# Entry to the scans of a state-space layer: sequences per statistics round, place of a table load, order of the silus

## Chip, cores and metric

The kernel runs on one core of a Trainium2 chip. The metric is the device time of one execution in microseconds, taken as the median of several runs. Engines are named as in the profile: PE (TensorE), DVE (VectorE), ACT (ScalarE), POOL (GpSimd) and SP (the queue that issues most DMAs).

## The reference, cut

16 sequences of 36 image tokens and 77 text tokens, 256 wide. Two layers: attention and a mixture of experts, then a state-space (scan) layer and a quantised feed-forward layer. The change lies where the scan layer begins:

```python
h = h + moe(_layernorm(h))            # L0_ffn: the expert answers are added here
x = _layernorm(h)
xr = x @ in_proj_w.T + in_proj_b
x_in, res = split(xr, 2)
xc = silu(causal_depthwise_conv(x_in, conv_w) + conv_b)      # 4 taps
delta, Bp, Cp = split(xc @ x_proj_w.T + x_proj_b, [64, 80])
delta = softplus(delta @ dt_proj_w.T + dt_proj_b)
dA, dBu = exp(delta * -exp(A_log)), delta * Bp * xc
ys = scan(dA * previous + dBu)                                # along time, 16 states
y = ((ys * Cp).sum(-1) + xc * D_param) * silu(res)
h = h + y @ out_proj_w.T + out_proj_b + x @ skip_proj_w.T + skip_proj_b
h = h + quantised_ffn(_layernorm(h))
```

## The kernel before, in words

Every engine has its own instruction stream, written out by hand, and the streams meet on semaphores; an engine runs its stream strictly in the order of the code. Whatever stands behind a waiting instruction on the same engine waits too.

The scan layer works in 8 groups of GB = 2 sequences (N = 226 columns), each group in 8 chunks of two states. After the experts, eight DMAs on SP bring the expert answers back into `xn2`, four sequences to a pair of DMAs and to a semaphore `gathered`. Then the entry begins:

- DVE (`dve_ssm`, from line 1199) quantises the last weights, then `add_answers` adds the answers of some sequences to `resid` and takes their statistics (lines 1203 and 1205, one pair per sequence); `dve_layernorm` (lines 837 to 852) makes mean and rstd out of them. It needs ACT in the middle: after seven operations ACT does Ln and Exp (`act_rstd`, lines 541 and 543), and then come four more on DVE. The first call covers FIRST_SEQS, four sequences. `normalise(0)` (line 1219) writes the two sequences of group 0 to `xn3`. Then the other twelve (OTHER_SEQS) are added, group 1 is normalised once PE has read group 0, and the second layernorm runs. `shift` (line 1285) is for ACT, which normalises the later groups itself.
- PE (`pe_ssm`) turns the group (L1644), projects it into x and then res (L1654, two halves), convolves x with diagonal matrices (L1664), projects xc to rank, B and C (L1673), and rank to dt (L1680). `spread` (L1691) copies B over the partitions, and `reduce` (L1704, L1709) adds what POOL multiplied.
- ACT (`act_ssm`) copies the turned group (L713), adds the bias into `xpad` (`pad`, L724), makes the silus of res (L733) and xc (L736) in `silus`, copies rank, B and C out (`projections`, L745 and L747), and makes softplus (L754 to L759) and the decays (L768). Silu and Exp/Ln lie in different tables. `silus` asks for the Exp/Ln table at its end (L739); the silu table is loaded in front of the first silu, where the profile shows it as line 733, behind the waits of `silus`.
- SP sends C to DRAM and back, spread over all partitions (`c_rows`, lines 414 and 418), once the second copy of `projections` is there; POOL splits B and C into three bfloat16 parts (L461 to L465) after the fourth, and multiplies states by C (L480, L484) in every chunk.
- DVE makes delta and delta * xc (`steps`, L1225, L1227), the drives (L1234) and the scans (L1244).

In each of the other groups this front work is woven into the chunks of the group before. Only for group 0 it stands alone, and for group 1 its convolution stands in chunk 1 of group 0 (OPENING). The streams of `act_ssm` and `dve_ssm` begin, before the change, like this:

```python
act: turn(0, 0); pad(0); silus(0, 0, first=True); projections(0, 0, first=True)
     act_rstd(act, 4, OTHER_SEQS, load=False); softplus(0); turn(1, 1)
dve: normalise(0); add_answers(OTHER_SEQS); wait_ge(x3T_ps, 1); normalise(1)
     dve_layernorm(dve, 4, OTHER_SEQS); shift; memset of the decays' first column; steps(0, 0)
```

After the scans the feed-forward layer follows: scale of x, rounding and turning, gate and up projections (L1620), scale of the hidden layer, down projections (L1634).

Of the kernel before, what the change touches and what calls it, by code (L numbers as in the profile page):

```python
# [18 lines left out]
B, IMG, TXT, D = 16, 36, 77, 256  # L19
# [19 lines left out]
GB = 2  # L39
# [12 lines left out]
AT_NORMALISE, AT_TURN, AT_IN, AT_PAD = 4, 5, 6, 7  # L52
OPENING = 1
AT_SKIP = (3, 4)
FIRST_SEQS, OTHER_SEQS = slice(0, 2 * GB), slice(2 * GB, B)
BUT_ONE_SEQS, ONE_SEQ = slice(0, B - 1), slice(B - 1, B)
ROUTER_BANKS = (0, 1, 3, 4)
TAIL_SEQS = 4
# [38 lines left out]
def build(nc, a, out):  # L97
    ctx = ExitStack()
    with ctx:
# [3 lines left out]
        def sem(name):  # L103
            return ctx.enter_context(nc.semaphore(name))
# [223 lines left out]
        xpad_ready, res_ready, conv_ps, xc_ready = sem("xpad_ready"), sem("res_ready"), sem("conv_ps"), sem("xc_ready")  # L328
# [207 lines left out]
        def act_rstd(act, turn, seqs=slice(0, B), load=True):  # L536

            if load:
                act.preload_act_table_set("natural_log_exp_and_others")
            act.wait_ge(dve_ln, LN_OPS * turn + LN_VAR)  # L540
            act.activation(lnt[:, 3, seqs], lnt[:, 2, seqs], ACT.Ln).then_inc(act_ln, 1)
            act.wait_ge(act_ln, 2 * turn + 1)
            act.activation(lnt[:, 3, seqs], lnt[:, 3, seqs], ACT.Exp, scale=-0.5).then_inc(act_ln, 1)
# [166 lines left out]
        def act_ssm(act):  # L710
# [10 lines left out]
            def pad(g):  # L721
                act.wait_ge(xin_ps, g + 1)
                for m in range(KT):
                    act.activation(xpad[:, m, :, TAPS - 1:], ps[:, 1, m * N:(m + 1) * N].rearrange("p (b s) -> p b s", b=GB),  # L724
                                   ACT.Identity, bias=in_b[:, m:m + 1]).then_inc(xpad_ready, 1)

            def silus(g, par, first=False):
                act.wait_ge(res_ps, g + 1)
                act.wait_ge(conv_ps, g + 1)
                if not first:  # L730
                    act.wait_ge(yT_ready, g)
                for m in range(KT):
                    act.activation(silu_res[par][:, m, :], ps[:, 0, m * N:(m + 1) * N], ACT.Silu, bias=in_b[:, KT + m:KT + m + 1])\  # L733
                        .then_inc(res_ready, 1)
                for m in range(KT):
                    act.activation(xc[par][:, m, :], ps[:, 1, m * N:(m + 1) * N], ACT.Silu, bias=conv_b[:, m:m + 1])\  # L736
                        .then_inc(xc_ready, 1)

                act.preload_act_table_set("natural_log_exp_and_others")  # L739

            def projections(g, par, first=False):
                act.wait_ge(proj_ps, g + 1)
                if not first:
                    act.wait_ge(c_out, 16 * g)
                act.activation(rankT, ps[0:RANK, 0, 0:N], ACT.Identity, bias=rank_b).then_inc(proj_ready, 1)  # L745
                for dst, rows in ((bc, 96), (bc_hi, 96), (bc3[par], 32)):
                    act.activation(dst[0:rows, :], ps[0:rows, 0, N:2 * N], ACT.Identity, bias=bc_b[0:rows, :]).then_inc(proj_ready, 1)  # L747

            def softplus(g):

                q = Seq(act, sp_step, 5 * g)
                act.wait_ge(dt_ps, g + 1)
                for m in range(KT):
                    q.done(act.activation(sp_abs[:, m, :], ps[:, 1, m * N:(m + 1) * N], ACT.Abs, bias=dt_b[:, m:m + 1]))  # L754
                for m in range(KT):
                    q.done(act.activation(sp_relu[:, m, :], ps[:, 1, m * N:(m + 1) * N], ACT.Relu, bias=dt_b[:, m:m + 1]))
                q.wait()
                q.step(act.activation(sp_abs, sp_abs, ACT.Exp, scale=-1.0))
                act.activation(sp_abs, sp_abs, ACT.Ln, bias=1.0).then_inc(softplus_ready, 1)  # L759
# [37 lines left out]
            turn(0, 0)  # L797
            pad(0)
            silus(0, 0, first=True)
            projections(0, 0, first=True)  # L800
            act_rstd(act, 4, OTHER_SEQS, load=False)
            softplus(0)
            turn(1, 1)
            act.wait_ge(aneg_done, 2)
# [10 lines left out]
        @block.scalar  # L815
        def _(act):
            act_tokens(act)
            act_rstd(act, 0)
            act.wait_ge(clip_in, 2 * 16)
            act.activation(clip_sig[:, :], clips[:, :], ACT.Exp, scale=-1.0).then_inc(clip_exp, 1)  # L820
            act_attention(act)
            act_router(act)
            act_shared(act)
            act_experts(act)
            act_weights_down(act)
            act_rstd(act, 3, FIRST_SEQS)
            act_ssm(act)
            act_rstd(act, 6, LAST_SEQS, load=False)
            act_ffn(act)
# [3 lines left out]
        def dve_layernorm(dve, turn, seqs=slice(0, B)):  # L833

            q = Seq(dve, dve_ln, LN_OPS * turn)
            me, qe, mo, qo = (stats[:, seqs, k] for k in (1, 2, 4, 5))
            q.done(dve.tensor_tensor(lnt[:, 0, seqs], me, mo, ALU.add))
            q.done(dve.tensor_tensor(lnt[:, 1, seqs], me, mo, ALU.subtract))
            q.done(dve.tensor_tensor(lnt[:, 2, seqs], qe, qo, ALU.add))
            q.wait()  # L840
            q.done(dve.tensor_scalar(mean[:, seqs], lnt[:, 0, seqs], 0.5, None, ALU.mult))
            q.done(dve.tensor_scalar(lnt[:, 2, seqs], lnt[:, 2, seqs], 1.0 / D, EPS, ALU.mult, ALU.add))
            q.step(dve.tensor_tensor(lnt[:, 1, seqs], lnt[:, 1, seqs], lnt[:, 1, seqs], ALU.mult))
            q.step(dve.scalar_tensor_tensor(out=lnt[:, 2, seqs], in0=lnt[:, 1, seqs], scalar=0.25, in1=lnt[:, 2, seqs], op0=ALU.mult, op1=ALU.add))
            assert q.n == LN_VAR

            dve.wait_ge(act_ln, 2 * turn + 2)
            y, v, t = lnt[:, 3, seqs], lnt[:, 2, seqs], lnt[:, 4, seqs]
            q.step(dve.tensor_tensor(t, y, y, ALU.mult))
            q.step(dve.tensor_tensor(t, t, v, ALU.mult))  # L850
            q.step(dve.tensor_scalar(t, t, -0.5, 1.5, ALU.mult, ALU.add))
            q.step(dve.tensor_tensor(rstd[:, seqs], y, t, ALU.mult))
            assert q.n == LN_OPS
# [345 lines left out]
        def dve_ssm(dve):  # L1199
            def add_answers(seqs):  # L1200
                for b in range(seqs.start, seqs.stop):
                    dve.wait_ge(gathered[b // 4], 32)
                    dve.tensor_tensor(resid[:, b, :], resid[:, b, :], xn2[:, b, :], ALU.add).then_inc(resid2_ready, 1)
                    dve.wait_ge(resid2_ready, b + 1)
                    dve.bn_stats(stats[:, b, :], resid[:, b, :]).then_inc(stats_done, 1)
                dve.wait_ge(stats_done, 2 * B + seqs.stop)
# [9 lines left out]
            def normalise(g):  # L1216
                for r in range(GB):
                    b = GB * g + r
                    dve.tensor_scalar(xn3[r], resid[:, b, :], mean[:, bass.ds(b, 1)], rstd[:, bass.ds(b, 1)],
                                      ALU.subtract, ALU.mult).then_inc(xn3_ready, 1)  # L1220
# [58 lines left out]
            dve.wait_ge(ey_ps, ETILES)  # L1279
            normalise(0)  # L1280
            add_answers(OTHER_SEQS)
            dve.wait_ge(x3T_ps, 1)
            normalise(1)
            dve_layernorm(dve, 4, OTHER_SEQS)
            dve.scalar_tensor_tensor(out=shift[:, :], in0=mean[:, :], scalar=-1.0, in1=rstd[:, :], op0=ALU.mult, op1=ALU.mult).then_inc(shift_ready, 1)
            dve.wait_ge(wqT_ready, 2 + 2 * FT + 4)
            for n in range(2):
# [13 lines left out]
        @block.vector  # L1301
        def _(dve):
            dve_tokens(dve)
            dve_layernorm(dve, 0)
            dve_attention(dve)
            dve_clips(dve)
            dve_router(dve)
            dve_shared(dve)
            dve_experts(dve)
            dve_ssm(dve)  # L1310
            dve_ffn(dve)
# [559 lines left out]
```

## Time and profile before

| | |
|---|---|
| median of 3 runs | 865.48 us (865.08 to 865.71) |
| the profiled execution | 865.44 us, span 863.5 us |
| mean granted TensorE clock | 0.89 of full speed |
| busy: PE, DVE, ACT, POOL | 699.7, 520.7, 392.2, 351.2 us |

The profile is one execution. Times in it are microseconds from the start of its span; the span is 1.9 us shorter than the execution's own time.
### The profile page before, as it was taken

What the parts mean: (1) busy time and instruction counts of PE and PEld (TensorE: products, weight loads), DVE (VectorE), ACT (ScalarE), POOL (GpSimd) and SP (SyncE); (2) the same over time, 40 slices, a digit from 0 to 9 for tenths busy, and PEclk for the clock granted to TensorE, in tenths of its full rate; (3) what the DMA queues carried; (4) which work ended last, traced back from release to release, by engine and by line L of the source; (5) the groups of instructions that cost most, each with busy time, mean ns of one, the idle gap of its engine ahead of it and who ended that gap; (6) DMA issues with size and microseconds to landing.
All of it is one profiled execution on the core that took longest, in us unless ns stands there. A gap on an engine that the chain in (4) does not pass through costs nothing. (4 is left out here: it accounts for less than half of the span.)

```text
span 863.5 us, 12104 instructions
## 1 busy us (share of the span) xinstructions
PE 699.7 (81%) x3696; PEld 474.2 (55%) x3697; DVE 520.7 (60%) x931; ACT 392.2 (45%) x858; POOL 351.2 (41%) x332
## 2 busy tenths in 40 slices
PE   7699999997999957999994788897788785535958
PEld 5577777775655524665663555455456452213557
DVE  1555555555231102544436568988988988974974
ACT  0465555554422103233222456665665662106973
POOL 0021111110035802323221158878878888420625
PEclk9899999997999968999997789999999997566955
DMA  9990000000002153111114202201210220000002
GB/s 274 335 416 20 0 0 0 0 2 0 1 7 39 31 104 114 44 49 43 43 36 98 88 1 87 87 29 59 86 54 34 87 87 0 0 0 1 0 11 76
DMA packets 28696, 52.73 MB, mean 61 GB/s; under 512 B 10965, under 2 KB 23545, under 8 KB 26489
## 3 DMA queue, kind: packets, MB, share of 16 engines
q1 hardware_dynamic: 19929, 47.49, 16.6%
q0 software_dynamic: 8736, 4.85, 2.2%
q8 instruction: 16, 0.26, 0.1%
q14 instruction: 15, 0.12, 0.0%
HBM read 42.62 MB, written 9.60 MB: 60 GB/s over the span
## 5 line engine op out<-in xcount | busy, mean ns | idle before, releaser
L480 POOL TENSOR_TENSOR arena<-arena 128x904 f32<-128x904 f32 x64 | 124.8, 1953 | 59.3 <-DVE arena L1244 53.0
L1244 DVE TENSOR_TENSOR_SCAN arena<-ps,arena 128x452 f32<-128x452 f32 x128 | 133.5, 1085 | 6.7 <-ACT ps L768 2.1
L768 ACT ACTIVATE ps<-arena,sh_w 128x448 f32<-128x448 f32 x128 | 80.3, 635 | 107.7 <-DVE arena L1244 106.9
L1704 PE MATMUL ps<-arena,const 128*128 128x452 f32 x112 | 63.2, 650 | 41.3 <-POOL arena L484 41.3
L554 ACT ACTIVATE work<-ps,work 113x113 f32<-113x113 f32 x256 | 67.1, 420 | 56.3 <-DVE work L899 56.3
L1528 PE MATMUL ps<-arena,work 128*128 x176 | 86.5, 618 | 0.3 <-issue 0.3
L428 POOL TENSOR_TENSOR xT<-work 128x452 f32<-128x452 f32 x16 | 15.1, 943 | 157.7 <-DVE work L888 157.7
L1234 DVE TENSOR_TENSOR arena<-arena,ps 128x904 f32<-128x904 f32 x64 | 69.2, 1082 | 11.1 <-PE ps L1691 10.7
L511 POOL DMA_INDIRECT slots_in<-xn,slot x16 | 37.9, 2366 | 74.1 <-issue 74.1
L484 POOL TENSOR_TENSOR arena<-arena 128x452 f32<-128x452 f32 x56 | 64.1, 1144 | 4.4
L527 POOL DMA_INDIRECT answers_e<-work,slot_token x22 | 23.7, 1076 | 101.5 <-DVE work L1033 101.5
L1496 PE MATMUL ps<-xT,sh_w 128*128 (+1 forms) x128 | 50.9, 556 | 0.0
L1029 DVE TENSOR_TENSOR work<-ps,work 128x512 f32<-128x512 f32 x22 | 15.2, 691 | 58.5 <-PE ps L1528 58.5
L1704 PEld LDWEIGHTS ps<-arena,const 128*128 128x128 f32 x112 | 19.2, 207 | 53.3 <-POOL arena L484 53.2
L1528 PEld LDWEIGHTS ps<-arena,work 128*128 128x128 f32 x176 | 31.5, 197 | 24.6 <-issue 24.4
L1540 PE MATMUL ps<-arena,work 128*128 x176 | 43.1, 389 | 0.8 <-ACT work L624 0.8
L1377 PE MATMUL ps<-const,work 113*113 113x113 f32 x256 | 37.4, 269 | 5.0 <-ACT work L554 4.7
L1654 PE MATMUL ps<-arena,sh_w 128*128 128x226 f32 x128 | 38.4, 462 | 0.7 <-ACT arena L713 0.7
L1496 PEld LDWEIGHTS ps<-xT,sh_w 128*128 128x128 f32 x128 | 24.9, 196 | 23.7 <-issue 23.2
L899 DVE TENSOR_REDUCE work<-ps 113x4 f32<-113x452 f32 x64 | 35.7, 620 | 2.8 <-PE ps L1371 2.8
L1377 PEld LDWEIGHTS ps<-const,work 113*113 113x113 f32 x256 | 31.6, 178 | 10.1 <-ACT work L554 8.8
L1540 PEld LDWEIGHTS ps<-arena,work 128*128 128x128 f32 x176 | 32.9, 197 | 5.3 <-issue 1.5
(239 smaller groups left out, 1428.5 us busy)
## 6 DMA issues: line engine op xcount, KB each, us to landing
arena<-c_rows SPq DMA_DIRECT2D x8, 1808.0 KB, 6.5
arena<-in_ex_w SPq DMA_DIRECT2D x8, 1536.0 KB, 23.6
slots_in<-work SPq DMA_DIRECT2D x1, 2827.0 KB, 22.3
work<-slots_in SPq DMA_DIRECT2D x22, 128.5 KB, 2.1
xn<-answers_e SPq DMA_DIRECT2D x4, 448.0 KB
out<-resid SPq DMA_DIRECT2D x8, 224.0 KB
arena<-in_patches SPq DMA_DIRECT2D x3, 576.0 KB, 6.0
sh_w<-in_sh_w SPq DMA_DIRECT2D x1, 1536.0 KB, 11.4
```

The lines of the kernel that those rows point to most:

```text
L480: pool.tensor_tensor(read[kp], state[kp], c_all[par][:, 2 * c:2 * c + 2, :].unsqueeze(2).broadcast_to([P, 2, KT, N]), ALU.mult)\
L484: pool.tensor_tensor(read[kp][:, 0], read[kp][:, 0], read[kp][:, 1], ALU.add).then_inc(pair_ready, 1)
L554: last = act.activation(probs[:, r, j], ps[0:S, 3 + r, j * S:(j + 1) * S], ACT.Exp, bias=negmax[:, h:h + 1])
L768: act.activation(decay_ps(n)[:, :, 1:], delta[par].rearrange("p k (b s) -> p (k b) s", b=GB)[:, :, 1:], ACT.Exp, scale=a_neg[:, 2 * c + n: ...
L1234: dve.tensor_tensor(drive[kp], dx[par].unsqueeze(1).broadcast_to([P, 2, KT, N]), ps[:, 2 + kp, 0:2 * N].rearrange("p (n s) -> p n s", n=2) ...
L1244: dve.tensor_tensor_scan(state[kp][:, n].rearrange("p k s -> p (k s)"), decay_ps(n).rearrange("p q s -> p (q s)"), drive[kp][:, n].rearran ...
L1377: last = pe.transpose(ps[0:S, 3 + r, j * S:(j + 1) * S], probs[:, r, j, :], ident[0:S, 0:S])
L1496: last = pe.matmul(ps[:, bank, 0:4 * S], sh_w[:, at + k * HID + m * P:at + k * HID + (m + 1) * P], xT2[:, k, bass.ds(g * 4 * S, 4 * S)], s ...
L1528: last = pe.matmul(ps[:, bank, :], xgT[par][:, k, :], arena[:, bass.ds(e * EW + at + k * HID, HID)], start=k == 0, stop=k == KT - 1)
L1540: last = pe.matmul(ps[:, 6, 0:D], e_hT[:, m, :], arena[:, bass.ds(e * EW + DOWN + m * D, D)], start=m == 0, stop=m == HT - 1)
L1654: last = pe.matmul(ps[:, 1 - m // KT, m % KT * N:(m % KT + 1) * N], in_w[:, k, m * P:(m + 1) * P], x3T[par][:, k, :], start=k == 0, stop=k ...
L1704: pe.matmul(ps[:, 6, 0:KT * N], ident, read[kp][:, 0].rearrange("p k s -> p (k s)"), start=False, stop=False, skip_group_check=True).then_ ...
```

## The change

FIRST_SEQS shrinks from four sequences to the two of group 0, and OTHER_SEQS grows to fourteen. In `silus` of group 0 alone, the silu table is asked for by an instruction of its own ahead of the waits, the silus of res wait for the res projection alone, and the wait for the convolution stands between them and the silus of xc. On ACT, Ln and Exp of the second layernorm move ahead of `projections(0)`. On DVE, the second layernorm moves ahead of `normalise(1)` and its wait.

```diff
-FIRST_SEQS, OTHER_SEQS = slice(0, 2 * GB), slice(2 * GB, B)
+FIRST_SEQS, OTHER_SEQS = slice(0, GB), slice(GB, B)
...
             def silus(g, par, first=False):
+                if first:
+                    act.preload_act_table_set("silu_and_others")
                 act.wait_ge(res_ps, g + 1)
-                act.wait_ge(conv_ps, g + 1)
                 if not first:
+                    act.wait_ge(conv_ps, g + 1)
                     act.wait_ge(yT_ready, g)
                 for m in range(KT):
                     act.activation(silu_res[par][:, m, :], ps[:, 0, m * N:(m + 1) * N], ACT.Silu, bias=in_b[:, KT + m:KT + m + 1])\
                         .then_inc(res_ready, 1)
+                if first:
+                    act.wait_ge(conv_ps, g + 1)
                 for m in range(KT):
                     act.activation(xc[par][:, m, :], ps[:, 1, m * N:(m + 1) * N], ACT.Silu, bias=conv_b[:, m:m + 1])\
                         .then_inc(xc_ready, 1)
...
             silus(0, 0, first=True)
+            act_rstd(act, 4, OTHER_SEQS, load=False)
             projections(0, 0, first=True)
-            act_rstd(act, 4, OTHER_SEQS, load=False)
             softplus(0)
...
             add_answers(OTHER_SEQS)
+            dve_layernorm(dve, 4, OTHER_SEQS)
             dve.wait_ge(x3T_ps, 1)
             normalise(1)
-            dve_layernorm(dve, 4, OTHER_SEQS)
```

## Rows read from the trace of the kernel before

**Rows 1.** The chain of waits around the stall; start us, us, what.

```profile
502.39 5.12 issue
...
512.36 2.10 DVE arena L1244 x2
...
514.52 1.95 POOL arena L480
```

**Rows 2.** The timeline, DVE, 462 to 516 us; start, us, engine, line, operation.

```profile
465.04 0.43 DVE L1203 TENSOR_TENSOR resid<-resid,xn 113x256 f32<-113x256 f32 x1 [2.95 <-DMA xn<-answers_e]
...
468.32 0.17 DVE L837 TENSOR_TENSOR lnt<-stats 113x4 f32<-113x4 f32 x1
...
469.75 0.16 DVE L849 TENSOR_TENSOR lnt<-lnt 113x4 f32<-113x4 f32 x1 [0.58 <-ACT lnt L543]
...
471.05 0.74 DVE L1219 TENSOR_SCALAR arena<-resid,mean,rstd 113x256 f32<-113x256 f32 x2 [0.54 <-DVE rstd L852]
...
480.80 0.43 DVE L1205 BATCH_NORM_STATS2 stats<-resid 113x6 f32<-113x256 f32 x1
...
482.66 0.17 DVE L844 SCALAR_TENSOR_TENSOR lnt<-lnt 113x12 f32<-113x12 f32 x1
...
495.81 2.09 DVE L1244 TENSOR_TENSOR_SCAN arena<-ps,arena 128x452 f32<-128x452 f32 x2
```

**Rows 3.** The timeline, PE, same stretch.

```profile
471.93 0.98 PE L1644 MATMUL ps<-const,arena 113*128 113x113 f32 x4 [6.51 <-DVE arena L1219]
...
479.20 3.22 PE L1664 MATMUL ps<-arena,xT 128*128 128x226 f32 x16
485.31 3.47 PE L1673 MATMUL ps<-arena,sh_w 128*64 128x226 f32 x8 [2.90 <-ACT arena L736]
489.32 1.03 PE L1680 MATMUL ps<-arena,sh_w 64*128 64x226 f32 x4 [0.54 <-ACT arena L745]
...
502.44 5.00 PE L1664 MATMUL ps<-arena,xT 128*128 128x226 f32 x16 [2.61 <-ACT arena L724]
...
510.33 1.92 PE L1673 MATMUL ps<-arena,sh_w 128*64 128x226 f32 x8 [0.40 <-ACT arena L736]
```

**Rows 4.** The timeline, ACT, same stretch.

```profile
477.03 0.79 ACT L724 ACTIVATE arena<-ps,sh_w 128x226 f32<-128x226 f32 x2 [3.47 <-PE ps L1654]
482.50 1.28 ACT L733 ACT_TABLE_LOAD   x1 [4.67 <-PE ps L1664]
...
484.47 0.79 ACT L736 ACTIVATE arena<-ps,sh_w 128x226 f32<-128x226 f32 x2
...
488.82 0.45 ACT L745 ACTIVATE arena<-ps,sh_w 64x226 f32<-64x226 f32 x1 [2.26 <-PE ps L1673]
...
490.17 0.19 ACT L541 ACTIVATE lnt<-lnt 113x12 f32<-113x12 f32 x1
...
490.51 0.77 ACT L754 ACTIVATE arena<-ps,sh_w 128x226 f32<-128x226 f32 x2
```

**Rows 5.** Busy time and granted clock by stretch (PEclk after the POOL column).

```profile
475.20:478.60 3.40, 3.40 (x10) 3.05 (x10) 3.23 (x10) 0.79 (x2) 0.00 (x0) 0.50 0.00 0
478.60:482.00 3.40, 3.40 (x19) 3.35 (x19) 3.26 (x10) 0.00 (x0) 0.00 (x0) 1.00 0.00 0
...
485.40:488.80 3.40, 3.39 (x8) 1.57 (x8) 0.00 (x0) 1.16 (x1) 0.00 (x0) 0.50 0.02 5
```

**Rows 6.** The transfers of C on SP's queue, all groups.

```profile
L418 SPq DMA_DIRECT2D arena<-c_rows x8: 338/338/348, 491.0 to 706.2; - x8
...
DMA to landing us min/median/max: 6.2/6.5/6.8
```

**Rows 7.** Busy time and clock by stretch, hidden layer and end.

```profile
791.70:796.00 4.30, 4.25 (x12) 2.33 (x13) 0.68 (x1) 3.12 (x5) 0.00 (x0) 0.50 0.02 4
796.00:809.70 13.70, 13.36 (x70) 7.96 (x68) 10.96 (x20) 13.42 (x24) 9.13 (x8) 1.00 0.00 1
...
823.40:858.00 34.60, 28.13 (x129) 27.52 (x130) 23.38 (x39) 21.50 (x12) 13.26 (x14) 0.50 0.14 41
```
## The prediction

> **What bounds the kernel now.** I read the chain of waits first. From 514.52 us on, the chain that ends last runs through POOL's products (L480) group after group, and ahead of that there are a few microseconds in which nothing else works: ACT idles 5.12 us until the convolution of group 1 is there, then loads tables and makes silus, and the scans go on at 512.36 [rows 1]. What this chain says for the change: from there on each step is released by the one before it, so whatever brings the first scan forward brings the end forward by as much, if the stall at 502 to 512 moves along. The view does not reach ahead of 502 in detail, so I read the entry (465 to 496 us) engine by engine in the order of time.
>
> DVE [rows 2]: answers of sequences 0 to 3 are added from 465.04; the layernorm over four begins at 468.32, group 0 is normalised at 471.05, twelve more sequences are added until 481.23, and the first seven operations of their layernorm end at 482.83. The first scan starts at 495.81. PE [rows 3]: turns group 0 from 471.93, after 6.51 idle, projects, convolves from 479.20, and waits 2.90 for ACT ahead of the x projection at 485.31. ACT [rows 4]: bias into xpad at 477.03, then 4.67 of idleness until the convolution, then table, four silus, table, and the four bc and rank copies from 488.82. So the entry is one serial path DVE, PE, ACT, PE, ACT, DVE, beside which DVE adds the other sequences. In such a stretch a removed link counts whole, as long as the work beside it is not late.
>
> **The change, part by part.** The entry's path before: 465.04 (add) to 468.32, layernorm, 471.93 (PE), 482.42 (convolution ends), 482.50 table, 483.78 silus of res, 484.47 silus of xc, 485.31 x projection, 488.82 copies, 490.51 softplus, 495.81 first scan.
>
> (a) *Two sequences instead of four.* Four cost 468.32 - 465.04 = 3.28, two leave 1.64 [rows 2]. The layernorm's operations are so small (0.17 for 4 columns, 0.17 for 12) that their width is worth nothing. Gain on the path 1.64. The two moved sequences join the others: 14 x 0.79 = 11.1 us from about 470.1, ending at 481.2, as before, because the normalising of group 0 comes earlier by just what the two cost. The answers wanted first (sequences 0 to 3) came at 465.0, when DVE first stopped waiting, and sequence 4 is wanted at 471.7, as before, so no load comes under pressure.
>
> (b) *The silu table while ACT waits.* The load of 1.28 at 482.50 [rows 4] goes behind the bias copies, which end at 475.4 + 0.8 = 476.2 (1.64 ahead of 477.03 + 0.79). The second half of the projection ends only at about 477.6, so the load is covered by PE. Gain 1.28. If the cover were gone it would cost at most these 1.28. The Trainium skill (ScalarE: Activation LUTs, What ACT_TABLE_LOAD costs) says a switch of set costs about 2.66 us, a drain of 1.38 beside the load of 1.28. The row shows 1.28 from the load's start to the first silu's, since ACT had long been empty; by the page the sum would be 1.38 larger, and the row decides.
>
> (c) *Silus of res during the convolution.* They run from 482.50 + 1.28 = 483.78 to 484.47: 0.69 off the path. They now need the second half of the projection alone and fit beside the 3.2 us of the convolution. They write nothing that it reads. Gain 0.69.
>
> (d) *Ln and Exp ahead of the copies instead of behind.* Before, they stood at 490.17 between the copies and softplus, while PE computed dt until 490.35; softplus began at 490.51. Freed, it can begin at about 490.40: gain 0.1. In the new place ACT waits for DVE's seventh layernorm operation, and behind that wait stand the copies, the SP queue's c_rows transfers, POOL's split of B and C, and softplus. DVE now skips the normalising of group 1 (0.65) before it: seventh operation at about 482.1. ACT gets there after xc (485.26 - 3.61 = 481.65) and the table back (1.28): 482.93. So ACT does not wait; Ln and Exp end at about 483.4, before the x projection (below, 483.6). Cost nothing, while DVE is not later than that.
>
> (e) *Group 1 normalised after the layernorm.* Four operations after Exp take 0.76 (469.75 to 470.51), normalising 0.74 and the 0.54 ahead of it: xn3 is ready near 485.5. PE wants it after dt, near 485.2. A delay of 0.3 there, covered: PE's next work for the scans (B spread over the partitions) waits for POOL's split anyway, 2.5 us more. Cost nothing.
>
> (f) *PE's clock.* Not in the diff, but the gaps between PE's bursts shrink. The granted clock was 1.00 (2.4 GHz) during the convolution, and 0.50 (1.2 GHz) in 485.40 to 488.80, after an idle time of 2.90 [rows 3, 5]. The same x projection shape takes 3.51 until its copy begins at half clock (485.31 to 488.82) and 1.92 later (510.33), which is the pace of the convolution at full clock, 3.22 for 16. With (b) and (c) the idle time ahead of it is 0.06 + 0.79 + 0.04 = 0.9 in place of 2.90; idle times as short as 0.54 ahead of dt left the clock full. Bounds: 0 (it falls all the same) and 1.92 against 3.47 = 1.55. I take 1.55, because 0.9 is much nearer to 0.54 than to 2.90. The projection into x and res ran at half clock from 473.6 to 478.6 [rows 5]; starting 1.64 sooner after the work that ended at 465.42 it may meet the rise at another place. Bounds by what was paid at half clock: 5.0 us at 0.50 cost 2.5, the convolution fully at half would cost 3.0 more. I take 0 and keep some of each.
>
> (g) *The transfer of C* is issued at 491.0 first and lands 6.5 us later [rows 6], 8.7 after the copies start at 488.82; the first scans end 495.81 + 2.09 - 488.82 = 9.1 after. It stays covered by a few tenths.
>
> (h) *The stall at 502 to 512.* Only the first group's order is changed, so it keeps its shape. Its convolution took 5.00 for 16 matmuls against 3.22 for the same 16 at full clock [rows 3]; at half throughout it would be about 6.2. So it can move by -1.8 to +1.2. I take 0.
>
> Sum: 1.64 + 1.28 + 0.69 + 0.10 + 1.55 = 5.26. The profiled execution took 865.44 us (span 863.5), 0.04 under the median of 865.48: **860.2 us**. What a measurement can tell from no change is about 0.2%, 1.7 us.
>
> **The rivals.**
> *Rigid shift.* The clock still falls ahead of the x projection, and (f) gives nothing: 3.7, 861.7 us. For it: what the clock had before is what one execution shows. Against: the short gap. The Trainium skill (TensorE: Matmul & The Clock Gate, Part 1) says that the instants at which activity is judged run free of the program, so other executions can meet them elsewhere; one trace cannot show that. Chance 0.22.
>
> *More clock, until DVE's statistics bind.* If the projection also gets its full clock sooner, the path reaches ACT's Ln before DVE does. Then the copies start at 482.1 + 0.45 = 482.6 at the earliest, 6.2 before 488.82: this is the cap, 6.3 with (d), 859.1 us; with a group 1 convolution at full clock too, up to 1.8 less, 857.3. Chance 0.25.
>
> *Given back.* The clock pattern shifts against the later work: the convolution of group 1 at half throughout (+1.2), or the hidden layer's first stretch, which ran 4.3 us at 0.50 and then at 1.00 [rows 7], rising one or two us later (+0.9). 3.7 - 2.1 = 1.6 gained: 863.8, no measurable change. Chance 0.08.
>
> *Slower.* The hidden layer's stretch from 796.0 to 809.7 ran at 1.00 with PE busy 13.36 of 13.70; the last stretch ran at 0.50 though PE was busy 28.13 of 34.60 [rows 7]. If the shift makes the first one stay at half as well, its 13.4 us of matmuls become 26.8: 865.4 - 5.3 + 13.4 = 873.5. It decides from 5.3 us of full-clock work done at half. For it: the last stretch shows that being busy is not enough. Against: the work itself, which set the rise, is the same. Chance 0.03.
>
> *It does not do what it says.* If a second silu load still stood before the silus, it would fall on those of res and be covered by the convolution (476.2 + 2.56 = 478.8, silus until 479.6, convolution until 480.8): nothing lost; this is inside the first cases.
>
> **How the numbers follow.** The sum as taken 0.42, rigid 0.22, cap 0.25, given back 0.08, slower 0.03. The likeliest gives the time, 860.2. Range 858.0 to 863.0: it takes in most of the cap's case and the rigid one with the conv at half, and leaves out the last two and the far end of the cap's. Faster by over 0.2% (below 863.7): 0.91; within: 0.06; slower: 0.03.
>
> **What would show it.** ACT: a table load right behind the bias copies, silus of res inside the convolution, no load between the convolution and xc. PE: idle under 1 us ahead of the x projection, and 1.7 to 2.0 us for its 8 matmuls. DVE: seventh layernorm operation at 482.0 to 482.3, and ACT's Ln not waiting for it. First scan near 490.6, the resumed scans near 507.1, and all of 514 to 863 shifted by the same. The prediction is wrong if Ln waits over 1 us for DVE, if the clock in the x projection is 0.50, or if the gain at the first scan differs from that at the end by over 1.5 us.

## The result, and the profile after

The change makes the kernel faster by half a per cent. Over 18 runs of each, 863.07 us median (858.09 to 865.01) against 866.75 (865.08 to 869.55), ratio 0.9949 with a 95% interval of 0.9936 to 0.9962, that is 4.4 us (3.3 to 5.5). The two medians are 3.7 apart, which lies in that interval too. The forecast was 5.26 us. Its 860.2 stood on the first three runs of the kernel before (865.48); carried over with the ratio, that is 865.48 x 0.9949 = 861.1. The median of the 18 runs itself lies 0.07 above the upper end of the forecast's range. Both kernels spread more than those three runs showed.

The profiled execution of the changed kernel took 860.82 us, span 859.0 (before: 865.44, span 863.5). ACT in the order of time at the entry, columns as in [rows 4]; lines behind 725 have moved by up to 4:

```profile
468.02 1.28 ACT L539 ACT_TABLE_LOAD   x1
469.32 0.20 ACT L541 ACTIVATE lnt<-lnt 113x2 f32<-113x2 f32 x1
...
477.53 0.79 ACT L724 ACTIVATE arena<-ps,sh_w 128x226 f32<-128x226 f32 x2 [3.47 <-PE ps L1658]
478.33 1.28 ACT L729 ACT_TABLE_LOAD   x1
479.63 0.79 ACT L735 ACTIVATE arena<-ps,sh_w 128x226 f32<-128x226 f32 x2
482.14 0.79 ACT L740 ACTIVATE arena<-ps,sh_w 128x226 f32<-128x226 f32 x2 [1.72 <-PE ps L1668]
482.94 1.28 ACT L743 ACT_TABLE_LOAD   x1
484.31 0.21 ACT L541 ACTIVATE lnt<-lnt 113x14 f32<-113x14 f32 x1
484.56 0.21 ACT L543 ACTIVATE lnt<-lnt 113x14 f32<-113x14 f32 x1
484.93 0.44 ACT L749 ACTIVATE arena<-ps,sh_w 64x226 f32<-64x226 f32 x1 [0.16 <-PE ps L1677]
...
486.49 0.79 ACT L758 ACTIVATE arena<-ps,sh_w 128x226 f32<-128x226 f32 x2
```

The table of silu is loaded right behind the bias copies, the silus of res (479.63) lie inside the convolution, and the silus of xc start 0.04 after it ends, with no load between. The rows below are PE of the same kernel, against [rows 3]:

```profile
472.42 0.99 PE L1648 MATMUL ps<-const,arena 113*128 113x113 f32 x4 [5.05 <-DVE arena L1223]
474.11 4.94 PE L1658 MATMUL ps<-arena,sh_w 128*128 128x226 f32 x16 [0.70 <-ACT arena L713]
478.88 3.22 PE L1668 MATMUL ps<-arena,xT 128*128 128x226 f32 x16
482.98 1.92 PE L1677 MATMUL ps<-arena,sh_w 128*64 128x226 f32 x8 [0.88 <-ACT arena L740]
485.43 1.03 PE L1684 MATMUL ps<-arena,sh_w 64*128 64x226 f32 x4 [0.53 <-ACT arena L749]
486.51 0.61 PE L1648 MATMUL ps<-const,arena 113*128 113x113 f32 x4
...
498.43 4.72 PE L1668 MATMUL ps<-arena,xT 128*128 128x226 f32 x16 [2.88 <-ACT arena L724]
```

The idle time ahead of the x projection is 0.88 instead of 2.90, and its 8 matmuls take 1.92 instead of 3.47. DVE, against [rows 2]:

```profile
466.54 0.43 DVE L1207 TENSOR_TENSOR resid<-resid,xn 113x256 f32<-113x256 f32 x1 [2.79 <-DMA xn<-answers_e]
...
468.92 0.16 DVE L848 SCALAR_TENSOR_TENSOR lnt<-lnt 113x2 f32<-113x2 f32 x1
...
471.54 0.74 DVE L1223 TENSOR_SCALAR arena<-resid,mean,rstd 113x256 f32<-113x256 f32 x2 [0.93 <-DVE rstd L856]
...
484.10 0.17 DVE L848 SCALAR_TENSOR_TENSOR lnt<-lnt 113x14 f32<-113x14 f32 x1
...
485.50 0.17 DVE L856 TENSOR_TENSOR rstd<-lnt 113x14 f32<-113x14 f32 x1
485.71 0.74 DVE L1223 TENSOR_SCALAR arena<-resid,mean,rstd 113x256 f32<-113x256 f32 x2
...
491.80 2.09 DVE L1248 TENSOR_TENSOR_SCAN arena<-ps,arena 128x452 f32<-128x452 f32 x2
```

Three things are new. Between the last operation of group 0's layernorm and its normalising DVE is idle for 0.93, not 0.54. Between the same two operations for group 1 (485.50, 485.71) there is only 0.04. And the seventh operation of the second layernorm ends at 484.27, 0.05 after ACT's table load (482.94 + 1.28 = 484.22) and 0.04 before ACT's Ln: ACT was already there, and DVE released it. The clock by stretch, against [rows 5] (granted clock after the POOL column): the projection's first 3.3 us at half, then full through the convolution and the x projection.

```profile
474.10:477.40 3.30, 3.29 (x9) 2.97 (x10) 3.13 (x10) 0.00 (x0) 0.00 (x0) 0.50 0.00 0
477.40:478.80 1.40, 1.40 (x9) 1.39 (x8) 1.36 (x4) 1.26 (x3) 0.00 (x0) 0.99 0.00 0
478.80:484.90 6.10, 5.22 (x26) 3.94 (x24) 5.19 (x20) 4.11 (x8) 0.00 (x0) 1.00 0.02 3
```

The differences of starts in the two profiles, step by step, are the whole balance:

| from, to | before | after | gained | forecast |
|---|---|---|---|---|
| first add, normalising of group 0 | 6.01 | 5.00 | 1.01 | 1.64 |
| normalising, projection | 2.56 | 2.57 | 0 | 0 |
| projection, convolution | 5.59 | 4.77 | 0.82 | 0 (bounds -3.0, +2.5) |
| convolution, x projection | 6.11 | 4.10 | 2.01 | 1.97 |
| x projection, copies | 3.51 | 1.95 | 1.56 | 1.55 |
| copies, softplus | 1.69 | 1.56 | 0.13 | 0.10 |
| softplus, first scan | 5.30 | 5.31 | 0 | 0 |
| **entry: first add, first scan** | **30.77** | **25.26** | **5.51** | **5.26** |
| first scan, resumed scans | 16.55 | 16.27 | 0.28 | 0 |
| resumed scans, end | 351.14 | 350.93 | 0.21 | 0 |

One more term lies ahead of the entry, where the code is the same: the first add came at 466.54 instead of 465.04, 1.50 later. 5.51 + 0.28 + 0.21 - 1.50 = 4.50, the difference of the spans.

The chain of waits after looks as in [rows 1], 4.3 us earlier (start us, us, what). So the gain of the entry passed through the stall into the scans:

```profile
498.38 4.84 issue
503.23 1.28 ACT L735
...
508.07 2.10 DVE arena L1248 x2
...
510.24 1.95 POOL arena L480
```

### The profile page after: what moved, and what is told of

It reads as the page before. It is cut to its first block and busy times, and to the rows that moved or that the text cites. A ratio compares the mean times of both kernels' runs of the same rounds, so it can differ in the third digit from the quotient of the medians.

```text
span 859.0 us, 12103 instructions
## 1 busy us (share of the span) xinstructions
PE 699.3 (81%) x3696; PEld 474.8 (55%) x3697; DVE 519.9 (61%) x931; ACT 393.1 (46%) x858; POOL 350.6 (41%) x332
## 5 line engine op out<-in xcount | busy, mean ns | idle before, releaser
L1658 PE MATMUL ps<-arena,sh_w 128*128 128x226 f32 x128 | 36.2, 440 | 0.7 <-ACT arena L713 0.7
```

## The experiments

The questions were: what each part is worth by itself, whether it is the idle time that takes PE's clock, why the first step fell short, and whether DVE's statistics are the next bound. The entry's length comes from one profile per run, with no noise from the code ahead of it. It is the sharper measure beside the times. "Filler" below means matmuls added on PE whose result is not used.

**e1_two_seqs.** The kernel before, with only the number of first sequences changed.

```diff
-FIRST_SEQS, OTHER_SEQS = slice(0, 2 * GB), slice(2 * GB, B)
+FIRST_SEQS, OTHER_SEQS = slice(0, GB), slice(GB, B)
```

> The kernel before with FIRST_SEQS = 2 sequences alone. The measure is the entry: from DVE's first add of answers to the first scan, 30.77 us before and 25.26 after the whole change. Theory (two sequences are 1.64 on the path): entry 29.1, time 1.6 below the kernel before. Rival (ACT's weight copies and its table load stand behind the same arrival and cap the gain, since the changed kernel went from the first add to group 0's normalising in 5.00 us against 6.01): entry 29.8, 1.0 below. The clock ahead of the x projection should be 0.50 again, 3.5 us for it.

Ratio 0.9991 (0.9974 to 1.0007), no measurable change. From the first add (464.93) to the normalising it took 4.80, and the entry took 30.30. DVE and PE:

```profile
469.73 0.73 DVE L1219 TENSOR_SCALAR arena<-resid,mean,rstd 113x256 f32<-113x256 f32 x2 [0.93 <-DVE rstd L852]
```

```profile
472.29 6.15 PE L1654 MATMUL ps<-arena,sh_w 128*128 128x226 f32 x16 [0.70 <-ACT arena L713]
...
484.39 3.08 PE L1673 MATMUL ps<-arena,sh_w 128*64 128x226 f32 x8 [2.90 <-ACT arena L736]
488.01 1.87 PE L1680 MATMUL ps<-arena,sh_w 64*128 64x226 f32 x4 [0.54 <-ACT arena L745]
```

The step paid 1.21, not 1.64, and of that PE's clock took most back. The whole projection ran at half (6.15 for 16 against 5.75 before) and so did dt (1.87 against 1.03), while the x projection came out 0.39 shorter; the entry kept 0.47. The rival blamed ACT's load. That load ended at 467.40, before DVE's seventh operation (467.47), and Ln started 0.03 after the latter, so the load was in time here and is not the cause. The missing 0.43 is, but for 0.04, the growth of the idle time from 0.54 to 0.93. The time alone can't tell the theory (1.6) from the rival (1.0).

**e2_silus.** The kernel before, with only the new `silus`: early table, silus of res ahead of the wait for the convolution.

```diff
+                if first:
+                    act.preload_act_table_set("silu_and_others")
                 act.wait_ge(res_ps, g + 1)
-                act.wait_ge(conv_ps, g + 1)
                 if not first:
+                    act.wait_ge(conv_ps, g + 1)
                     act.wait_ge(yT_ready, g)
...
+                if first:
+                    act.wait_ge(conv_ps, g + 1)
```

> The kernel before with the table asked for early and the silus of res during the convolution, four first sequences kept, and Ln/Exp and layernorm in their old places. Theory (removed 1.28 + 0.69 on ACT, and PE's clock stays full in the x projection, 1.55 more): entry 27.2 us, idle time ahead of the x projection 0.9 and 1.92 for its 8 matmuls, time 3.5 below. Rival (the clock gain needs the earlier start too): x projection 3.5, entry 28.8, 2.0 below.

Ratio 0.9968 (0.9946 to 0.9990), 2.8 us. Entry 27.49. PE:

```profile
483.71 3.22 PE L1668 MATMUL ps<-arena,xT 128*128 128x226 f32 x16
487.80 1.92 PE L1677 MATMUL ps<-arena,sh_w 128*64 128x226 f32 x8 [0.88 <-ACT arena L740]
```

From the convolution to the x projection it took 4.09 against 6.11, and the clock gain of 1.55 comes with this part alone: the theory holds. The entry is 0.3 longer than expected, since the projection took 5.89 to the convolution, not 5.59.

**e3_both.** The change without its two moves of the second layernorm.

```diff
             silus(0, 0, first=True)
-            act_rstd(act, 4, OTHER_SEQS, load=False)
             projections(0, 0, first=True)
+            act_rstd(act, 4, OTHER_SEQS, load=False)
...
-            dve_layernorm(dve, 4, OTHER_SEQS)
             dve.wait_ge(x3T_ps, 1)
             normalise(1)
+            dve_layernorm(dve, 4, OTHER_SEQS)
```

> The change without its two moves of the second layernorm (Ln/Exp stay behind the copies, DVE's layernorm behind the normalising of group 1). Theory (those moves are worth 0.1): entry 25.3 to 25.5, time 4 to 5 below the kernel before. Rival (the moves bring DVE's statistics onto the path, so without them it is faster, since the changed kernel's Ln began only 0.04 after DVE's seventh operation): entry below 25.1.

Ratio 0.9953 (0.9937 to 0.9970), 4.1 us. Entry 26.60, longer than the 25.3 to 25.5 expected. The projection accounts for it: 6.05 to the convolution against 4.77. From the x projection to the first scan it took 8.93, the changed kernel 8.82, so the moves pay 0.11 as forecast, and the rival, that they cost something here, fell.

**e4_filler.** The kernel before, with a filler of 7 matmuls in PE's idle time ahead of the x projection.

```diff
             convolve(0)
+            for _ in range(7):
+                pe.matmul(ps[:, 6, 0:N], in_w[:, 0, 0:P], x3T[0][:, 0, :], start=True, stop=True, skip_group_check=True)
             project_x(0, 0)
```

> The kernel before with 7 matmuls of 128x226 more on PE between the convolution and the x projection, into a PSUM bank that nothing uses yet: PE has work in the 2.90 us of idleness, nothing on the path is removed. Theory (the idle time makes the clock fall, and that costs 1.55): x projection 1.9 us at clock 1.00, entry 29.2, time 1.5 below. Rival (the clock falls for another reason, or the filler delays PE): x projection 3.5, entry 30.8 or more, time no less than before.

Entry 29.55, x projection at 1.92:

```profile
480.83 3.22 PE L1664 MATMUL ps<-arena,xT 128*128 128x226 f32 x16
483.89 2.83 PE L1768 MATMUL ps<-arena,sh_w 128*128 128x226 f32 x14
486.94 1.92 PE L1673 MATMUL ps<-arena,sh_w 128*64 128x226 f32 x8 [0.23 <-ACT arena L736]
```

With nothing removed, work in the idle time alone keeps the clock: 1.55 less in this step. That the idle time takes the clock at this place is shown: after 2.90 of it the 8 matmuls took 3.47 and 3.08 (two profiles), after 0.88 or with the filler 1.92 (twelve profiles). As a time it is not shown: ratio 0.9987 (0.9963 to 1.0010). In this profile the convolution of group 1 took 5.95 instead of 5.00, and the last output projection was slow too (below, f4_opening).

**f1_early.** The changed kernel with DVE's five semaphore increments ahead of the last weights, and ACT's Exp/Ln table ahead of its four weight copies.

```diff
+            for counted in (state_ready, read_ready, read_used, drive_ready):
+                dve.sem_inc(counted, 2)
+            dve.sem_inc(yT_ready, 1)
             dve_weights_down(dve)
             add_answers(FIRST_SEQS)
             dve_layernorm(dve, 3, FIRST_SEQS)
-            for counted in (state_ready, read_ready, read_used, drive_ready):
-                dve.sem_inc(counted, 2)
-            dve.sem_inc(yT_ready, 1)
...
+            act.preload_act_table_set("natural_log_exp_and_others")
             act_weights_down(act)
-            act_rstd(act, 3, FIRST_SEQS)
+            act_rstd(act, 3, FIRST_SEQS, load=False)
```

> The changed kernel, with the Ln/Exp table asked for ahead of ACT's four weight copies and DVE's five semaphore increments moved ahead of the last weights. In every run with two first sequences so far DVE went from the first add to the normalising of group 0 in 4.8 to 5.0 us instead of the 4.37 forecast (6.01 - 1.64): 0.93 of idleness ahead of the normalising instead of 0.54, and ACT's Ln up to 0.24 behind DVE. Theory (the increments and the table load are what stands there): 4.4 us from the first add to the normalising, entry 0.5 shorter than in the changed kernel at the same clock, time 4.9 below the kernel before. Rival (the 0.93 is something else, the start of an instruction after a wait): 4.7 to 4.9, no shorter.

Ratio 0.9914 (0.9894 to 0.9934) to the kernel before, 7.5 us. Entry 24.52; the first add came at 463.98. DVE, then ACT:

```profile
467.77 0.16 DVE L857 TENSOR_TENSOR rstd<-lnt 113x2 f32<-113x2 f32 x1
467.96 0.73 DVE L1224 TENSOR_SCALAR arena<-resid,mean,rstd 113x256 f32<-113x256 f32 x2
```

```profile
466.56 0.20 ACT L541 ACTIVATE lnt<-lnt 113x2 f32<-113x2 f32 x1 [1.40 <-DVE lnt L849]
```

From the first add to the normalising it took 3.98 in place of 4.80 to 5.00: not just the 0.39 that had been lost came back, the 0.93 shrank to 0.03. ACT now waits 1.40 for DVE. The two edits were not run apart; in g1_change, below, ACT already waited 0.43 for DVE with the load in its old place and the step still took 4.80, so 0.8 of the gain is the increments'. It fits that the changed kernel, too, has only 0.04 between layernorm and normalising for group 1, where no increments stand. The time fell by more than the 4.9 expected. The entry is 6.25 shorter than before, which the interval (5.7 to 9.2) holds; a gain beyond the entry is not shown.

**f2_warm.** f1_early with a filler ahead of turning group 0.

```diff
             pe.wait_ge(wqT_ready, 2 + 2 * FT + 4)
+            for _ in range(8):
+                pe.matmul(ps[:, 6, 0:N], in_w[:, 0, 0:P], in_w[:, 1, 0:N], start=True, stop=True, skip_group_check=True)
             turn(0, first=True)
```

> The run f1_early with 8 matmuls more on PE (128x226, a free PSUM bank) behind the wait for ACT's weight copies, ahead of turning group 0. Theory (the projection in runs at half clock because PE idled 5 us before it; DVE's fourteen sequences then bind): from the start of the projection to the convolution 3.3 us instead of 4.8 to 6.1, ACT's Ln waits 1 to 2 us for DVE, copies start with Exp's end, entry near 24.6, time 5.5 below. Rival (the filler does not lift the clock, or delays PE): 5.5 to 6.1 and no gain.

Ratio 0.9932 (0.9910 to 0.9954). Entry 24.82. PE, then ACT:

```profile
466.39 3.29 PE L1769 MATMUL ps<-sh_w 128*128 128x226 f32 x16 [0.78 <-ACT dq L658]
...
471.08 3.33 PE L1659 MATMUL ps<-arena,sh_w 128*128 128x226 f32 x16 [0.70 <-ACT arena L713]
...
496.45 6.37 PE L1669 MATMUL ps<-arena,xT 128*128 128x226 f32 x16 [2.92 <-ACT arena L724]
```

```profile
481.74 0.21 ACT L541 ACTIVATE lnt<-lnt 113x14 f32<-113x14 f32 x1 [2.16 <-DVE lnt L849]
...
482.11 0.43 ACT L749 ACTIVATE arena<-ps,sh_w 64x226 f32<-64x226 f32 x1
```

The projection now takes 3.17 to the convolution, and what the prediction called the cap happens: Ln waits 2.16 for DVE's fourteen sequences, and the copies behind it start 1.85 after the x projection has ended. While ACT waits, PE idles 2.34, and dt then takes 1.87, its time at half clock. Nothing is gained over f1_early.

**f3_warm_ln_late.** f2_warm with Ln and Exp back behind the copies (ACT's lines as in the diff of e3_both; DVE's layernorm stays ahead).

> The run f2_warm with ACT's Ln and Exp back behind the copies. Theory (with a fast projection the Ln ahead of the copies is on the path, so putting it behind pays 1 to 1.5): entry near 23.3, time 6.5 below the kernel before. Rival (the clock was not lifted, the order of Ln makes 0.1 as in e3_both): entry 25 to 26, within 0.2 of f2_warm.

Ratio 0.9877 (0.9859 to 0.9896). Entry 22.54, 2.28 less than f2_warm; in that profile the first add came as late as 468.20. ACT:

```profile
483.50 0.44 ACT L749 ACTIVATE arena<-ps,sh_w 64x226 f32<-64x226 f32 x1 [0.71 <-PE ps L1678]
483.85 1.09 ACT L751 ACTIVATE arena<-ps,sh_w 96x226 f32<-96x226 f32 x3
484.95 0.21 ACT L541 ACTIVATE lnt<-lnt 113x14 f32<-113x14 f32 x1
```

Ln behind the copies waits for nobody, though by little: DVE's seventh operation ended at 484.92, the copies at 484.94. With a fast projection, the place that the change chose for Ln costs over 2 us of the entry.

**f4_opening.** f1_early with a filler of 6 matmuls on PE ahead of the convolution of group 1.

```diff
+                        if not before and c == OPENING:
+                            for _ in range(6):
+                                pe.matmul(ps[:, 7, 0:N], in_w[:, 0, 0:P], x3T[1][:, 0, :], start=True, stop=True, skip_group_check=True)
                         if c == (AT_CONV if before else OPENING):
                             convolve(g + 1)
```

> The run f1_early with 6 matmuls more on PE between the projection and the convolution of group 1, in the 2.9 us in which PE waits for the bias into xpad. That convolution took 5.0, 4.7, 5.0, 5.0, 5.0 and 5.95 us in the six profiles so far, 3.22 at full clock. Theory (the idle time makes the clock fall): convolution 3.3 us, from the first scan to the resumed scans 14.8 instead of 16.5, time 6.5 below. Rival (PE had been at half clock during the projection, and the filler only adds to the queue ahead of the convolution): 16.5 or more, no gain over f1_early.

Ratio 0.9934 (0.9910 to 0.9957): no gain over f1_early. Yet the convolution took 3.32, and from the first scan to the resumed scans it was 14.87. From there to the end it took 353.26 against 351.20 in f1_early. Most of the difference is in the last output projection, in f4_opening and then in f1_early:

```profile
766.81 3.72 PE L1730 MATMUL ps<-sh_w,arena 128*113 128x256 f32 x8 [0.72 <-DVE arena L1255]
```

```profile
765.40 1.98 PE L1730 MATMUL ps<-sh_w,arena 128*113 128x256 f32 x8 [0.72 <-DVE arena L1255]
```

The granted clock there, in the same order:

```profile
766.80:770.50 3.70, 3.69 (x8) 2.31 (x8) 0.00 (x0) 0.00 (x0) 0.00 (x0) 0.52 0.00 0
```

```profile
765.40:767.40 2.00, 1.98 (x8) 1.33 (x8) 0.00 (x0) 0.00 (x0) 0.00 (x0) 1.00 0.00 0
```

So the 1.53 won ahead of the scans (16.40 to 14.87) was lost behind them, 1.74 of 2.06 at a place that no edit had touched. Of fourteen profiles three had the slow one (e4_filler, f2_warm, f4_opening). All three are among the six with a filler somewhere, none among the eight without. g4_best_opening, with the same filler as here, did not have it, so this filler does not bring it about by itself; whether fillers make it likelier is not shown. Nor is it shown that the filler made the convolution of group 1 fast: g2_early_ln_late and g3_best_again, below, have 3.32 without a filler directly ahead of it.

**g1_change.** This is the changed kernel again.

> The changed kernel itself, once more and on the same chip as the three others, for a second profile of it. Theory (what a run gains hangs on where PE's clock rises in the projection and in the convolution of group 1): from the first add to the normalising 4.8 to 5.0 again, the x projection 1.92 again, entry between 24.8 and 26.6 by the place where the clock rises, time 4.4 below the kernel before within 1.5. Rival (a fixed loss besides): entry as in the first profile to 0.1, and the projection to the convolution 4.8 again.

Ratio 0.9944 (0.9923 to 0.9966), 4.9 us. The entry took 25.40: from projection to convolution 5.12 instead of 4.77, from first add to normalising 4.80 instead of 5.00. The variation of the projection is the clock's, and the fixed loss is in the 0.93, which is there again. The 0.20 between 4.80 and 5.00 is ACT: in the first profile its load ended at 469.30 and Ln had to wait for it, here Ln waited 0.43 for DVE.

**g2_early_ln_late.** f1_early with Ln behind the copies, no filler.

> The run f1_early with Ln and Exp behind the copies, without filler. It tells what the move of Ln is worth where the projection runs at half clock. Theory (there ACT reaches Ln about when DVE has the numbers, the two orders differ by 0.1 to 0.3): entry 24.4 to 24.8, time within 1 of f1_early, 0.991 to 0.993 of the kernel before. Rival (Ln behind the copies is what made f3_warm_ln_late fast, with or without the filler): 0.988.

Ratio 0.9916 (0.9889 to 0.9942), as f1_early's 0.9914; entry 24.88. With the slow projection (5.05 to the convolution) the place of Ln is worth nothing measurable in time. In the entry Ln behind the copies costs 0.36 against f1_early (24.52), a little more than expected: softplus began 0.12 later behind the copies, and the first scan another 0.24, with PE waiting 3.03 for DVE's normalising of group 1 ahead of the spread of B. So the gain of f3_warm_ln_late needs both edits.

**g3_best_again.** f3_warm_ln_late again, beside the changed kernel.

> The run f3_warm_ln_late once more, against the changed kernel on the same chip. Theory: entry 22.5 again, since with the filler the projection is at full clock wherever the clock's changes fall; time 3 to 5 below the changed kernel. Rival (its 0.988 was luck of the chip): within 2 of the changed kernel.

Ratio 0.9884 (0.9858 to 0.9911), median 857.98 against 862.76 of the changed kernel on the same chip. Entry 22.53. The convolution of group 1 took 3.32 here, as in g2_early_ln_late, with no filler directly ahead of it and after a longer idle time than the 2.61 before which it took 5.00 in the kernel before:

```profile
494.84 3.32 PE L1669 MATMUL ps<-arena,xT 128*128 128x226 f32 x16 [3.00 <-ACT arena L724]
```

**g4_best_opening.** This is the same kernel with the filler of f4_opening.

> The run f3_warm_ln_late with the 6 matmuls of f4_opening as well. Theory (the convolution of group 1 at full clock pays 1.5 at the resumed scans, and the tail after the scans gives back up to 1.8 or not by where the clock changes fall there): first scan to resumed scans 14.9, time 0 to 1.5 below g3_best_again. Rival (the filler itself costs later): slower than g3_best_again by 0.5 or more.

Ratio 0.9871 (0.9843 to 0.9899), median 856.78; entry 22.54, first scan to resumed scans 14.86. The difference to g3_best_again (1.2 us) is inside the intervals, and its profile took 857.10 against 856.26. It is not shown to be better, nor worse. Either version beats the kernel before by 10 to 11 us and the changed kernel by about 5 to 6.

## Why the prediction was right, and where it was not

**The chain, and what it says.** Right. What came off the entry passed through the stall into the scans and to the end: 5.51 at the first scan, 5.79 at the resumed scans, 6.00 at the end, counted from the first add.

**(a), two sequences.** Mis-sized: 1.01 and 1.21 in the two profiles of the change and 1.21 in e1_two_seqs, against 1.64. The 3.28 for four sequences was read rightly; what was missed is that the 0.54 of idleness behind the layernorm [rows 2] was not a constant. It holds five semaphore increments of DVE, written between layernorm and normalising and named in no row. With two first sequences it grew to 0.93, and with the increments elsewhere it was 0.03 (f1_early). Why it grew by 0.39 was not found. A second, small part is ACT's table load, up to 0.24 late in the first profile, which the prediction did not look at for the first layernorm.

**(b) and (c), table and silus.** Right: 2.01 against 1.97, and e2_silus alone gives 2.02. ACT's rows show the early load at 1.28, 0.01 behind the bias copies, with the next operation 0.02 behind it (478.33 to 479.63). The Trainium skill (ScalarE: Activation LUTs, What ACT_TABLE_LOAD costs) counts a further 1.38 of drain for every switch. These rows do not show it, and not because ACT had long been empty, which was the prediction's reason: here it had just worked.

**(d), Ln and Exp.** Right in size (0.13 against 0.10, 0.11 in e3_both), but with none of the margin that was given: forecast was 0.8 of slack between DVE's numbers (482.1) and ACT's arrival (482.93), and in the first profile ACT was there 0.05 before the numbers. Counted from the first add, DVE's numbers came 0.67 later than forecast, nearly all of it by what (a) lost, and ACT 0.21 sooner. With the slower projection of g1_change DVE was ready 0.31 ahead of ACT. The sign given for DVE (482.0 to 482.3) was missed: taking off the 1.50, it was 482.77. The prediction named the price of being late there, and f2_warm shows it: 2.16 of waiting.

**(e), (g).** The outcome was as forecast: group 1 was turned at 486.51 right behind dt, and POOL's first product followed the first scans. One size in (e) was wrong: it put the 0.54 ahead of the normalising of group 1 as well, and there it was 0.04.

**(f), PE's clock.** The 1.55 was right, and its cause is shown from both sides: the idle time shortened (e2_silus) and filled (e4_filler). It is no rule for every gap: ahead of the convolution of group 1, 3.00 of idleness left the clock full in g3_best_again and 2.36 in g2_early_ln_late, while 2.57 to 4.04 in other kernels came with 4.7 to 6.4 for the same matmuls. The projection was taken at 0 and gave 0.82 and 0.47; in the other kernels without the filler ahead of it, it took between 5.05 and 6.05. This term is a spread and not a number.

**(h), the stall.** 0.28 against 0. Across the fourteen profiles the convolution of group 1 took from 3.32 to 6.37, close to the bounds given (3.2 and 6.2). The 0.28 is as much chance as the 0 was.

**The rivals.** Rigid shift fell with the x projection at 1.92 in all profiles that have the new `silus`. The cap is real, and binds with a projection at full clock. Given back happened in part in e4_filler, f2_warm and f4_opening, none of them the change: at the last output projection (1.74 in f4_opening), a place the prediction had not priced, and in e4_filler and f2_warm at the convolution of group 1 (5.95 and 6.37) too. The hidden layer, from its first projection to the first down projection, took 40.24 before and 40.17 after: the slower case did not come. In sum, (a) was forecast 0.6 too high and the projection 0.8 too low, and the two met within the entry: that its 5.51 stands so near 5.26 is in part luck. The time came 0.9 short of the forecast. The code ahead of the entry explains this at least in the profile, since it ended 1.50 later there; by the intervals 5.26 is inside 3.3 to 5.5. Whether anything systematic is left in those 0.9 us stays open.

## What to carry to other kernels

Ahead of a single serial path, look up what every idle piece between two instructions of one engine holds: semaphore increments do not show as work, and here moving them paid 0.8 us, as much as one sequence of the statistics. A wait moved ahead of work that others need is free only at the speed at which the rest runs now: this one had between nothing and 0.3 us left and cost 2 as soon as PE was faster. And where PE idles 3 us ahead of a burst of matmuls, unused matmuls in the gap can bring the burst to full clock; whether the total gains must be measured over many runs, because later bursts can run slower, as the last output projection did in three of the six kernels with a filler.

## What was not expected of the hardware

The first is where the entry begins. With the same code ahead of it, the first answers were added between 464.85 and 469.25 us in seven profiles (before, change twice, e1 to e4), as wide a spread as that of the runs of the kernel before. The transfer of the answers is not what spreads. DVE's rows of the same code lie 1.65 later in the changed kernel and 3.89 later in e2_silus than in the kernel before as early as 341 us, and 1.50 and 4.21 later at the first add; the profiles part between 200 and 341 us, and the cause is open.

The second is that the same 16 matmuls of group 1's convolution took 3.32, 4.7 to 5.0, 5.95 or 6.37 us, the 3.32 both with and without a filler directly ahead of them. f3_warm_ln_late and g3_best_again are one and the same kernel, with 5.01 and 3.32. The Trainium skill (TensorE: Matmul & The Clock Gate, Part 1) says that activity is judged on a grid of time that runs free of the program. These two profiles of one kernel agree with that.
